# Distance attention: the running sum gets a ring of its own, and the steps of a pair of heads move to other slots

## What is computed

```python
scores = jnp.einsum('bhid,bhjd->bhij', qh, kh) / jnp.sqrt(jnp.float32(DH))
s_ = jnp.where(maskb, scores, -1e+32)
p = jax.nn.softmax(s_, axis=-1) * maskb.astype(scores.dtype)
cum = jnp.cumsum(p, axis=-1)
tot = jnp.sum(p, axis=-1, keepdims=True)
pos = jnp.abs(idx[None, :] - idx[:, None])
dist_scores = jnp.sqrt(jnp.clip((tot - cum) * pos, 0.0, None))
gamma = -jax.nn.softplus(gammas)[None]
diff = jnp.exp(jax.nn.sigmoid(pdiff))[:, None]
total_effect = jnp.clip(jnp.exp(dist_scores * gamma * diff), 1e-05, 100000.0)
scores = jnp.where(maskb, scores * total_effect, -1e+32)
scores = jax.nn.softmax(scores, axis=-1)
scores = scores.at[:, :, 0, :].set(0.0)
return jnp.einsum('bhij,bhjd->bhid', scores, vh)
```

## Time and profile before

| | us |
|---|---|
| median of 3 runs | 3425.42 (3422.04 to 3426.59) |
| the profiled execution: its own time | 3424.7 |
| its span, first to last instruction | 3422.8 |
| the loop and its unrolled ends, about | 2500 to 3322 |

### The profile page before, as it was taken

One profiled execution on the slowest core, in us unless ns is written; L12 is line 12 of the kernel. 1 busy time (PEld: TensorE's weight loads), 2 busy tenths in 40 slices (PEclk: granted clock), 3 DMA queues, 4 the chain that ended last, 5 costly groups with the idle time before them and its releaser, 6 DMA issues. The chain is left out here.

```text
span 3422.8 us, 48765 instructions
## 1 busy us (share of the span) xinstructions
PE 2789.1 (81%) x14898; PEld 1568.8 (46%) x14992; DVE 1958.6 (57%) x4849; ACT 1730.3 (51%) x2836; POOL 804.4 (24%) x911
## 2 busy tenths in 40 slices
PE   5899849969999997657699799998667777777777
PEld 2333249934444444323222359996324343343443
DVE  6577641155555555107788521114678888888853
ACT  2366511136555554101377423331469889889953
POOL 2000020020000000001100030003357777777740
PEclk8899969979999999788899999999779999999998
DMA  4111136520000000892122239994410000000001
GB/s 159 38 52 45 46 128 209 197 85 1 1 1 1 1 1 15 354 425 77 60 57 61 85 145 351 345 343 136 155 19 19 19 21 13 25 18 9 25 24 51
DMA packets 160959, 326.54 MB, mean 95 GB/s; under 512 B 29360, under 2 KB 128432, under 8 KB 137136
## 3 DMA queue, kind: packets, MB, share of 16 engines
q1 hardware_dynamic: 156208, 312.13, 26.1%
q0 software_dynamic: 4608, 12.59, 1.1%
HBM read 275.22 MB, written 49.28 MB: 95 GB/s over the span
## 5 line engine op out<-in xcount | busy, mean ns | idle before, releaser
L3135 DVE TENSOR_TENSOR_SCAN L3x_fade<-L3x_first_exp,L3x_scores 128x513 f32<-128x513 f32 x256 | 311.5, 1217 | 48.1 <-PE L3x_probs_tp L2945 47.0
L3016 POOL TENSOR_TENSOR L3x_fade<-L3x_fade,L3x_apart 128x1024 f32<-128x1024 f32 x128 | 278.9, 2179 | 196.6 <-DVE L3x_mx L3153 157.7
L2942 PE MATMUL L3x_probs_tp<-identity,L3x_fade 128*128 128x128 f32 x1024 | 163.6, 283 | 177.4 <-ACT L3x_probs_T L3081 143.6
L1430 ACT ACTIVATE L1x_probs<-L1x_scores,L1x_neg_max 128x512 f32<-128x512 f32 x256 | 173.5, 683 | 226.6 <-DVE L1x_neg_max L1484 226.6
L2942 PEld LDWEIGHTS L3x_probs_tp<-identity,L3x_fade 128*128 128x128 f32 x1024 | 113.9, 142 | 281.2 <-issue 140.2
L1484 DVE TENSOR_REDUCE L1x_neg_max<-L1x_scores 128x2 f32<-128x1024 f32 x128 | 156.7, 1224 | 142.9 <-PE L1x_scores L1319 142.9
L1824 ACT ACTIVATE L2f_hiddenT<-L2f_hidden_ps,L2f_b1s 128x128 f32<-128x128 f32 x320 | 99.9, 363 | 208.3 <-PE L2f_hidden_ps L1759 208.3
L3053 ACT ACTIVATE L3x_first_exp<-L3x_scores,L3x_nm 128x512 f32<-128x512 f32 x256 | 175.4, 685 | 54.2 <-DVE L3x_nm L3127 52.6
L930 DVE CUSTOM_DVE_ANT_0 L0x_masked_scores<-L0x_s,L0x_mask_q 128x512 f32<-128x512 f32 x256 | 167.0, 685 | 57.6 <-issue 57.5
L3061 ACT ACTIVATE L3x_fade<-L3x_fade,L3x_tiny,L3x_rl 128x512 f32<-128x512 f32 x256 | 194.4, 814 | 0.0
L925 DVE TENSOR_REDUCE L2x_neg_max<-L2x_s 128x1 f32<-128x512 f32 x256 | 164.7, 685 | 36.5 <-PE L2x_s L819 36.0
(11 more groups left out here) (522 smaller groups left out, 6174.9 us busy)
## 6 DMA issues: line engine op xcount, KB each, us to landing
...
```

What stands on the lines that cost most here:

```text
L1430: nc.scalar.activation(p[:, n % 3, h, :], s[:, n % 2, h, :], ACT.Exp, bias=nmax[:, n % 4, h:h + 1], accum_out=den[:, n % 4, h:h + 1]).then ...
L2942: nc.tensor.matmul(tp[:, kt, :], fz[:, f, kt * P:(kt + 1) * P], c.ident[:], start=(kt == 0), stop=False, is_transpose=True)
L3016: nc.gpsimd.tensor_tensor(fz[:, f:f + 2, 0:S], fz[:, f:f + 2, 0:S], w, ALU.mult).then_inc(y_done, 1)
L3135: nc.vector.tensor_tensor_scan(fz[:, f, :], ex[:, t, :], sA[:, t, 0:1].to_broadcast([P, S + 1]), 0.0, ALU.add, ALU.bypass).then_inc(f_done, 1)
```

## The change

- The scan writes to a new ring `bs` of 8 tiles, and POOL's `distance` reads `bs` and writes `fz`. The wait for `turn_faded` moves from the scan (DVE) to `distance` (POOL); the scan waits instead for the `distance` that read its `bs` tile two units before. `fz` loses its 513th column; `share` reads `bs`.
- `turned_copy` moves from O1 to O2 (after `last_exp`), `turn_back` from O2 to slot 0 of the next even body, and `outputs` from O3 to that body too, cut in three: `invert` in E1, `keep_rows` in E2, `outputs` in E3. `values` runs one body later. One more unrolled body at the end.
- `log` has no bias; the 1e-18 it added is now the first element of `ex`, and distances are at least 1e-15.
- The batch's rows go to a part of `c.ctxT`, which is no longer read by then.

```diff
...
         nmp = c.sb(ctx, tag + "neg_max_parts", [P, F, 2], BF16)
 
         ex = c.sb(ctx, tag + "first_exp", [P, TB, S + 1], F32)
-        fz = c.sb(ctx, tag + "fade", [P, F, S + 1], F32)
-        tiny = c.sb(ctx, tag + "tiny", [P, 1], F32)
+        bs = c.sb(ctx, tag + "behind", [P, 2 * TB, S + 1], F32)
+        fz = c.sb(ctx, tag + "fade", [P, F, S], F32)
         gate = c.sb(ctx, tag + "gate", [P, TB], F32)
         pT = c.sb(ctx, tag + "probs_T", [P, 4, TB, S], F32)
         vst = c.sb(ctx, tag + "v_pair", [P, 2, TB, 2, PW], F32)
...
         oT = c.sb(ctx, tag + "o_turned", [P, S], F32)
         amr = c.sb(ctx, tag + "all_masked_row", [P, TB, P], F32)
         rdm = c.sb(ctx, tag + "rdm", [P, TB, 2], F32)
-        osb = c.sb(ctx, tag + "o_batch", [P, 2 * TB, HD], F32)
+        osb = c.ctxT[:, 0, :].rearrange("p (t d) -> p t d", d=HD)
         sA = c.ps(ctx, tag + "scores", [P, TB, 512], F32)
         sB = c.ps(ctx, tag + "scores_again", [P, 2, 512], F32)
         tp = c.ps(ctx, tag + "probs_tp", [P, TB, P], F32)
...
             with eng.Fori(1, 7) as r:
                 for i in range(8):
                     body(r * 8 + i, i, r * 4 + i // 2)
-            for k in range(56, U + 4):
+            for k in range(56, U + 5):
                 body(k, k % 8, k // 2)
 
         def there(u):
...
                         u, iu, tt = tile_at(k, i, t, 8)
                         if there(u):
                             first_scores(u, iu, tt)
-                        if i % 2 and there(k + (-4)):
-                            if t == 0:
-                                weigh(g + (-2), i // 2 % 2)
-                            elif t == 2:
-                                turn_back(g + (-2), i // 2 % 2)
+                        if i % 2 and t == 0 and there(k + (-4)):
+                            weigh(g + (-2), i // 2 % 2)
+                        if i % 2 == 0 and t == 0 and there(k + (-5)):
+                            turn_back(g + (-3), (i // 2 + 1) % 2)
 
                 for t in range(TB):
                     last = nc.tensor.transpose(op[0:1, t * P:(t + 1) * P], am[:, t:t + 1], c.ident[:])
...
                                             ).then_inc(clip2_done, 1)
 
                 def distance(u, i, half):
-                    f = (i % 4) * TB + 2 * half
+                    f, fb = (i % 4) * TB + 2 * half, (i % 2) * TB + 2 * half
                     pool.wait_ge(f_done, u * TB + (2 * half + 2))
+
+                    wait_pos(pool, t_done, u * TB + (2 * half + 2 - F))
                     w = apart[:, ds((u // H) * TB + 2 * half, 2), :]
-                    nc.gpsimd.tensor_tensor(fz[:, f:f + 2, 0:S], fz[:, f:f + 2, 0:S], w, ALU.mult).then_inc(y_done, 1)
+                    nc.gpsimd.tensor_tensor(fz[:, f:f + 2, :], bs[:, fb:fb + 2, 0:S], w, ALU.mult).then_inc(y_done, 1)
 
                 def max_parts(u, i, half):
                     f = (i % 4) * TB + 2 * half
...
                 def body(k, i, g):
                     if there(k + (-1)):
                         pool.wait_ge(eff_done, k)
-                    if there(k + (-2)):
-                        values(k + (-2), (i - 2) % 8, g + (-1))
+                    if there(k + (-3)):
+                        values(k + (-3), (i - 3) % 8, g + (-1 if i % 2 else -2))
                     if there(k + (-1)):
                         clip(k + (-1), (i - 1) % 8)
                     for half in range(2):
...
                     act.wait_ge(y_done, u * 2 + (half + 1))
                     act.wait_ge(rl_done, u * 2 + (half + 1))
                     for f in range((i % 4) * TB + 2 * half, (i % 4) * TB + 2 * half + 2):
-                        nc.scalar.activation(fz[:, f, 0:S], fz[:, f, 0:S], ACT.Ln, bias=tiny[:], scale=rl[:, f:f + 1]
+                        nc.scalar.activation(fz[:, f, 0:S], fz[:, f, 0:S], ACT.Ln, scale=rl[:, f:f + 1]
                                              ).then_inc(ln_done, 1)
 
                 def root(u, i):
...
                         u, iu, tt = tile_at(k, i, t, -12)
                         if there(u):
                             last_exp(u, iu, tt, g + (-1 if i % 2 else -2))
-                        if t == 1 and i % 2 and there(k + (-4)):
+                        if t == 2 and i % 2 and there(k + (-4)):
                             turned_copy(g + (-2))
                         if there(k):
                             if t < 2:
...
                 for h in range(2):
                     nc.vector.tensor_tensor(pick[:, h, :], c.ident[:, 2 * h * PW:2 * h * PW + VW],
                                             c.ident[:, (2 * h + 1) * PW:(2 * h + 1) * PW + VW], ALU.add)
-                nc.vector.memset(ex[:, :, 0:1], 0.0)
-                nc.vector.memset(tiny[:], 1e-18).then_inc(cleared, 1)
+                nc.vector.memset(ex[:, :, 0:1], 1e-18).then_inc(cleared, 1)
                 dve.wait_ge(cleared, 1)
                 dve.wait_ge(am_turned, 1)
                 nc.vector.tensor_copy(amr[0:1, :, :].rearrange("p t q -> p (t q)"), op[0:1, :]).then_inc(am_ready, 1)
...
                                             ).then_inc(m_done, 1)
 
                 def behind(u, i, t):
-                    f = (i % 4) * TB + t
+                    f = (i % 2) * TB + t
                     dve.wait_ge(e_done, u * TB + (t + 1))
 
-                    wait_pos(dve, t_done, u * TB + (t + 1 - F))
-                    nc.vector.tensor_tensor_scan(fz[:, f, :], ex[:, t, :], sA[:, t, 0:1].to_broadcast([P, S + 1]), 0.0,
+                    wait_pos(dve, y_done, u * 2 + (t // 2 - 3))
+                    nc.vector.tensor_tensor_scan(bs[:, f, :], ex[:, t, :], sA[:, t, 0:1].to_broadcast([P, S + 1]), 0.0,
                                                  ALU.add, ALU.bypass).then_inc(f_done, 1)
 
                 def share(u, i, half):
 
-                    f = (i % 4) * TB + 2 * half
+                    f, fb = (i % 4) * TB + 2 * half, (i % 2) * TB + 2 * half
                     dve.wait_ge(f_done, u * TB + (2 * half + 2))
-                    nc.vector.reciprocal(rl[:, f:f + 2], fz[:, f:f + 2, S]).then_inc(rl_done, 1)
+                    nc.vector.reciprocal(rl[:, f:f + 2], bs[:, fb:fb + 2, S]).then_inc(rl_done, 1)
 
                 def faded(u, i, t):
                     f = (i % 4) * TB + t
...
                     nc.vector.tensor_scalar(fz[:, f:f + 2, 0:S], fz[:, f:f + 2, 0:S], 1e-5, None, ALU.max
                                             ).then_inc(clip_done, 1)
 
-                def outputs(g):
+                def invert(g):
 
                     dve.wait_ge(o_done, g + 1)
                     nc.vector.reciprocal(rdm[:], o4[:, :, :, dk]).then_inc(rd_done, 1)
+
+                def keep_rows(g):
                     dve.wait_ge(rd_done, g * 2 + 1)
                     nc.vector.tensor_tensor(rdm[:], rdm[:], row_mask[:].unsqueeze(2).to_broadcast([P, TB, 2]), ALU.mult
                                             ).then_inc(rd_done, 1)
+
+                def outputs(g):
                     dve.wait_ge(rd_done, g * 2 + 2)
                     b, h = g // 8, (g % 8) * 2
 
...
                         u, iu, tt = tile_at(k, i, t, 4)
                         if there(u):
                             behind(u, iu, tt)
-                        if t == 3 and i % 2 and there(k + (-4)):
-                            outputs(g + (-2))
+                        if i % 2 == 0 and there(k + (-5)):
+                            if t == 1:
+                                invert(g + (-3))
+                            elif t == 2:
+                                keep_rows(g + (-3))
+                            elif t == 3:
+                                outputs(g + (-3))
                         u, iu, tt = tile_at(k, i, t, -8)
                         if there(u):
                             faded(u, iu, tt)
...
     d["pdiff"] = a(i["fside_BxSxS2_0"].reshape(N, S)[:, ::-1])
     d["gammas"] = i["L3_xattn_gammas"].reshape(H)
     at = np.arange(S, dtype=np.float32)
-    d["distance"] = np.abs(at[:, None] - at[None, ::-1])
+    d["distance"] = np.maximum(np.abs(at[:, None] - at[None, ::-1]), np.float32(1e-15))
     first = np.ones(S, np.float32)
     first[0] = 0.0
     d["row_mask"] = cols(first)
```

## The result

The changed kernel is slower: 3444.8 us (median of 18 runs, 3432.34 to 3455.14) against 3427.95 (18 runs, 3421.26 to 3436.37) of the kernel before on the same chip, a ratio of 1.0049, 95% interval 1.0038 to 1.0059. The profiled execution took 3440.18 us, its span is 3438.3, 15.5 more than before.

What follows compares the result with a forecast made beforehand. A ring of waits, no full engine, was taken to bound the kernel. Pairs falling from 24.81 to 24.0 us gave 20 us in the loop, plus 2 at the start: 22 off 3424.7, so 3402 us, range 3355 to 3420.

Steps and rivals of the forecast that it cites:

- What bounds the kernel: In the pair loop no engine is full; a ring of waits sets the pace, 24.81 us a pair.
- What the change removes: Per pair: the scan's wait, up to 1.5 us; the copy's 1.10 for `weigh`; ACT's 1.18 in E0.
- The ring walk of 23.85 us: The new order's steps from E2's first exp round to the next, with waits of 0.6 and 1.2 us on ACT.
- the 22 us: Whole forecast saving off the profiled 3424.7 us: 20 in the loop's 24 pairs, 2 at the start.
- the 24.0 of my sum: Forecast us per pair in the new order, with `keep_rows` held 0.15, against 24.81 in the loop before.
- `keep_rows`, held about 0.15: On DVE in E2, beside POOL's first multiplication: held about 0.15 us a pair, bounds 0 and 2.4.
- rival (c): No gain: holds of `keep_rows` and the clips cost 0.7 us a pair more, 3420 us; chance 0.12 shared with no effect.
- The logarithm, 2 us at the start only: ACT's logs 0.105 us shorter without bias; nothing in steady state, 2 us from the five bodies before the first `weigh`.
- At nothing: Items costed at zero, among them `distance`'s wait for the turning, the scan's new wait, later `values` and the extra body.
- rival (d): Slower: POOL's multiplication holds DVE's clip of E3 in full, 1.6 us, 25.6 a pair, 3450 us; chance 0.08.
- the signs I had named: Profile signs: copies 24.0 us apart and the forecast waits if right; copies under 23, long clip or `keep_rows` if wrong.

Runs made afterwards that it cites:

- E3: Not a run: slot 3 of the even body in a pair, where the changed kernel has `outputs`; no measured time of its own.
- b_moves: The kernel before with only the pair's steps moved apart, scan and logarithm as they were: ratio 1.0053 to the kernel before, stage 766.5 us.
- a_quarter_inv2: The changed kernel with loads by two units, `keep_rows` in E3 and the inversion in E2: ratio 0.9863 to the kernel before, stage 708.7 us.
- b_ring: The kernel before with only the scan's eight tiles, `distance` waiting for the turning and outputs in `ctxT`: ratio 0.9999 to the kernel before.
- a_quarter_keep: The changed kernel with loads by two units instead of four and `keep_rows` in E3: ratio 0.9918 to the kernel before, stage 729.9 us.
- a_quarter: The changed kernel with loads by two units instead of four: ratio 0.9961 to the kernel before, stage 740.0 us.
- c_split: The changed kernel, loads by two units, inversion in E2, `keep_rows` between E3's clip and scan, outputs behind the scan: ratio 0.9835 to the kernel before.

## Why the prediction was wrong

I predicted 3402 us, range 3355 to 3420, with 0.8 on faster. It is slower by 0.5%. Step by step:

- **What bounds the kernel**, a ring of waits through `weigh`, `turn_back`, inversion and `maxima`: supported. With the scan's waits in place the moves shorten the pair (b_moves, 24.61 where no load is late, against a mean of 24.99 before; E3's clip is free there as well, 0.69), and taking the inversion's wait away shortens it again (a_quarter_inv2). b_ring gains nothing without the scan's wait, but with longer clips, so it fits and proves little.
- **What the change removes**: right as to the waits. The scan and the copy wait for nothing, and E0's first exponential has no wait of 1.2. What the scan's wait was worth is not shown: the moves alone (766.5) and the whole change (767.2) have the same stage, and no run has the new order without its two costs and the scan as before.
- **The ring walk of 23.85 us**: its two forecast waits are there, 0.66 before the last exponential of O2 (I had 0.6) and, in the short pair, 1.73 at the inversion (1.6) and 1.49 at the first exponential of E2 (1.2). With the two costs below removed the pair is 24.23, so the walk was 0.2 to 0.4 short, in the wait of E2 above all. The saving came out near the 22 us, a_quarter_keep's stage being 21.3 below that of before, and that is partly luck: the pair is 0.2 longer than the 24.0 of my sum, and I counted from 24.81 where the mean of the loop was 24.99 before, with the loop's turn, which costs nothing any more (pairs of 24.20 to 24.27).
- **`keep_rows`, held about 0.15**: failed. I took POOL's first multiplication to end 9.48 us after the `faded` of slot 3, as it did before. But POOL's body waits for the `faded` of slot 1, and I had myself put a wait of 1.6 us (the inversion) just ahead of that `faded`. The multiplication slides with it, and `keep_rows`, one slot later, always meets it: in the short pair the multiplication ends 10.18 us after that `faded` (2956.59 to 2966.77) and `keep_rows` comes at 9.09, where I had 9.48 and 9.3. So it is held 1.0 instead of 0.15. Cost by the stage: 740.0 - 729.9 = 10 us, 0.35 in each pair of the loop. It lay between my bounds of 0 and 2.4, and rival (c) had the mechanism with 0.7 a pair.
- **The loads**: not in the sum at all, not even among what I cost at nothing. Their wait was absent before, and I didn't ask how nearly. It had 0.7 us of slack in a stretch of PE that held `turn_back`; moving `turn_back` took 1.7 out. Cost with what it does to the clock: 767.2 - 740.0 = 27 us, the largest term.
- **The clock**: taken at 1.00 as in the earlier trace rows. After waits of 1.48, 1.02 and 1.04 us within 7 us it falls to 0.50 over just those products that the inversion waits for. 13 of the 27 us. The waits alone don't explain it: 1.48, 1.02 and 1.00 us left the clock at 1.00 one pair with a load later.
- **The logarithm, 2 us at the start only**: on the kernel before it gives 0.2%, about 7 us. My "nothing" for the steady state was about the new order, where no run took it away. One logarithm became 74 ns shorter (814 to 740), less than my bound of 105.
- **At nothing**: `distance`'s wait for the turning. In b_ring it is 21.5 us in 400, beside longer clips; in the changed kernel 8.0, in a_quarter 2.2, so there it was rightly left out. The clip of E3, rival (d), is free, as I had it. That O3's clip, free before, would be held instead (0.69 to 1.56) I had nowhere; ACT's first exponential of E0 behind it has no wait, so it costs the ring nothing in these pairs.

Against the signs I had named: the copies were to be 24.0 apart and are 24.56 at best; the long `keep_rows`, my sign for (c), is there; no sign spoke of a load.

The sum by stage lengths: -21 for the change freed of its new costs, +10 for the hold, +27 for loads and clock, together the +16 between 751.2 and 767.2. The ratios, which rest on all executions, give -28, +15 and +30, each to some 7 us.

Settled by runs: that the moves carry the loss, that it is made of the loads, the clock and the hold, and about how much each costs. Open: what the scan's own tiles are worth in the new order; why the clock falls in one of two pairs with a late load and not in the other, and in some pairs of a_quarter_inv2 but in none of c_split.
